# Block-diagonal products of the recurrent stage as 64x64 quarters, two blocks side by side

## What is computed

```python
def _layernorm(x, axis=-1, eps=1e-05):
    m = jnp.mean(x, axis=axis, keepdims=True)
    v = jnp.var(x, axis=axis, keepdims=True)
    return (x - m) / jnp.sqrt(v + eps)

xp = jnp.einsum('tbi,hi->tbh', x_in, W_ih) + b_ih + b_hh      # x_in = _layernorm(h)
def step(h, xp_t):
    h_new = jnp.tanh(xp_t + h @ W_hh.T)
    return (h_new, h_new)
...
h = h + _L1_attn_ref(_layernorm(h, axis=-1), ...)   # the recurrence
h = h + _L1_ffn_ref(_layernorm(h, axis=-1), ...)    # slice attention: logits, softmax, z, o
```

## Time and profile before

| | |
|---|---|
| median of 3 runs | 3429.57 us (3427.73 to 3431.83) |
| profiled execution | 3429.93 us, span 3428.1 us |
| busy: TensorE, VectorE, ScalarE, GpSimd | 88%, 74%, 63%, 58% of the span |
| TensorE's granted clock, mean | 0.953 of 2.4 GHz |
| stage of the change | about 1950 to 3428 us |

### The profile page before, as it was taken

How to read it: one execution, slowest core, us unless ns; L and a number is a source line. 1 busy time by engine, 2 the same in 40 slices (tenths; PEclk the granted TensorE clock), 3 DMA queues, 4 the chain that set the end, 5 groups by cost and what they waited for, 6 DMA issues and landing times. The chain is left out here.

```text
span 3428.1 us, 66757 instructions
## 1 busy us (share of the span) xinstructions
PE 3002.8 (88%) x24922; PEld 1681.2 (49%) x24922; DVE 2535.4 (74%) x3280; ACT 2168.8 (63%) x3082; POOL 1989.1 (58%) x1191
## 2 busy tenths in 40 slices
PE   8999999969898888974699758899999999999997
PEld 6777777735555555542244323344444444444444
DVE  7888888868888888872487447776767777777773
ACT  5666666658777777751244346676766666666662
POOL 7777777712788888886100256565656565655531
PEclk9999999989999999995899879999999999999999
DMA  1111111111212212111444311111111111111102
GB/s 45 39 39 40 39 39 39 35 53 44 62 55 68 58 52 58 53 40 38 156 150 150 114 36 34 32 52 45 52 46 51 46 51 46 51 47 47 48 26 52
DMA packets 208262, 191.09 MB, mean 56 GB/s; under 512 B 76381, under 2 KB 163398, under 8 KB 207562
## 3 DMA queue, kind: packets, MB, share of 16 engines
q1 hardware_dynamic: 173850, 142.95, 14.2%
q0 software_dynamic: 25600, 26.01, 3.0%
q10 hardware_dynamic: 8496, 17.87, 1.4%
HBM read 99.08 MB, written 87.65 MB: 54 GB/s over the span
## 5 line engine op out<-in xcount | busy, mean ns | idle before, releaser
L2363 POOL TENSOR_TENSOR E_w<-E_w,E_rs 128x1024 f32<-128x1024 f32 x200 | 409.0, 2045 | 528.6 <-DVE E_rs L2271 528.6
L2356 POOL DMA_INDIRECT E_row<-yb,P_gi x400 | 391.1, 978 | 399.2 <-POOLq L93 305.4
L647 POOL DMA_INDIRECT xb<-B_yt,P_gi x400 | 523.3, 1308 | 120.8 <-issue 114.1
L203 POOL TENSOR_TENSOR A_kmask<-A_ksb,A_pack_a 128x3584 f32<-128x3584 f32 x56 | 356.5, 6365 | 151.1 <-ACT A_ksb L350 151.1
L2256 DVE TENSOR_REDUCE E_mx<-E_lg 128x16 f32<-128x1024 f32 x200 | 242.3, 1211 | 203.5 <-PE E_lg L1919 198.7
L2155 ACT ACTIVATE E_w<-E_w 128x1024 f32<-128x1024 f32 x200 | 211.5, 1057 | 281.8 <-DVE E_w L2264 238.4
L2268 DVE TENSOR_REDUCE E_sm<-E_w 128x16 f32<-128x1024 f32 x200 | 243.8, 1219 | 121.4 <-ACT E_w L2155 110.2
L1950 PEld LDWEIGHTS E_wt<-S_pack_f,E_w 128*128 128x128 f32 (+1 forms) x1600 | 173.1, 143 | 198.6 <-issue 136.3
L432 DVE COPY A_vbd<-A_v 128x512 f32<-128x512 f32 x392 | 248.6, 680 | 15.2 <-PE A_v L290 15.0
L1950 PE MATMUL E_wt<-S_pack_f,E_w 128*128 128x128 f32 (+1 forms) x1600 | 220.9, 282 | 38.5 <-ACT E_mo L2203 25.9
L2264 DVE TENSOR_TENSOR E_w<-E_lg,E_mx 128x1024 f32<-128x1024 f32 x200 | 244.8, 1224 | 6.7
(11 more groups left out here) (322 smaller groups left out, 6972.3 us busy)
## 6 DMA issues: line engine op xcount, KB each, us to landing
R_xs<-xb SPq DMA_DIRECT2D x57, 256.0 KB, 2.7
yb<-R_ys SPq DMA_DIRECT2D x57, 256.0 KB, 2.0
B_x<-h SPq DMA_DIRECT2D x25, 512.0 KB
h<-B_hh SPq DMA_DIRECT2D x25, 512.0 KB
A_xg<-in_xw SPq DMA_DIRECT2D x56, 224.0 KB, 2.9
h<-A_res ACTq DMA_DIRECT2D x56, 224.0 KB, 2.0
E_hx<-h SPq DMA_DIRECT2D x48, 256.0 KB
out<-E_ob SPq DMA_DIRECT2D x96, 128.0 KB
```

The costliest lines, as they stand in the source:

```text
L203: nc.gpsimd.tensor_tensor(kmask[i % 2][:], bc(ksb[i % 2][:].unsqueeze(2), [128, J, H, Q]), bc(head_of_row[:].unsqueeze(1).unsqueeze(3), [1 ...
L647: pool.indirect_dma_start(out=xb, out_offset=bass.IndirectOffsetOnAxis(ap=routed.gi[0:k, c, b:b + 1], axis=0), in_=yt[c % LT][0:k, D * row ...
L2356: pool.indirect_dma_start(out=row[b % LR][:, k, i], out_offset=None, in_=yb, in_offset=bass.IndirectOffsetOnAxis(ap=idx[:, c, 2 * n + i:2 ...
L2363: TT(w3, w3, bc(rs[g % 3][:].unsqueeze(2), [128, 2 * SH, G]), ALU.mult).then_inc(w_done, 1)
```

## The change

`center_in(s)` and `inputs(s-1)` become one step, `center_and_inputs(s)`, and `variance(s)` and `variance_out(s-2)` become `variances(s)`. Each 128x128 product is issued as two 64x64 products on the quarters that are not zero. `along` takes rows i of the array to columns i, `across` takes rows i to columns 1-i, so that the result's halves are swapped; the centering of block s is issued across, its squares lie swapped in `sr`, and the variance, across again, puts them back. Both blocks' quarters are issued alternately, across to PI and along to PO. All semaphore waits of a joined step stand ahead of its first matmul. `center_and_inputs` stands ahead of product or turn_back, where `center_in` and `inputs` stood behind them; `first_hidden` stays behind them and gets a wait for `ih_done`.

```diff
-                def center_in(b):
-                    pe.wait_ge(x_done, b + 1)
-                    mm(PI[:, 0:wide(b)], center, x[b % LX][:, 0:wide(b)], start=True, stop=True).then_inc(cen_done, 1)
+                def across(i, to, weights, b, data, **kw):
+                    return mm(to[HALF[1 - i], 0:wide(b)], weights[HALF[i], HALF[i]], data[HALF[i], 0:wide(b)],
+                              start=True, skip_group_check=True, **kw)
+
+                def along(i, to, weights, b, data, **kw):
+                    return mm(to[HALF[i], 0:wide(b)], weights[HALF[i], HALF[i]], data[HALF[i], 0:wide(b)],
+                              start=True, skip_group_check=True, **kw)
+
+                def center_and_inputs(b):
+                    first, second = 0 <= b < BLOCKS, 0 <= b - 1 < BLOCKS
+                    if first:
+                        pe.wait_ge(x_done, b + 1)
+                    if second:
+                        pe.wait_ge(y_done, b)
+                        after(pe, hc_done, b - 1)
+                    for i in range(2):
+                        if first:
+                            cen = across(i, PI, center, b, x[b % LX], stop=True)
+                        if second:
+                            ih = along(i, PO, wih, b - 1, sr, stop=b - 1 < J)
+                    if first:
+                        cen.then_inc(cen_done, 1)
+                    if second:
+                        ih.then_inc(ih_done, 1)
...
-                def variance(b):
-                    pe.wait_ge(sq_done, b + 1)
-                    after(pe, yk_done, b - 2)
-                    mm(PI[:, 0:wide(b)], mean, sr[:, 0:wide(b)], start=True, stop=True).then_inc(var_done, 1)
-
-                def inputs(b):
-                    pe.wait_ge(y_done, b + 1)
-                    after(pe, hc_done, b)
-                    mm(PO[:, 0:wide(b)], wih, sr[:, 0:wide(b)], start=True, stop=b < J,
-                       skip_group_check=True).then_inc(ih_done, 1)
+                def variances(b):
+                    first, second = 0 <= b < BLOCKS, 0 <= b - 2 < BLOCKS
+                    if first:
+                        pe.wait_ge(sq_done, b + 1)
+                        after(pe, yk_done, b - 2)
+                    if second:
+                        pe.wait_ge(sq2_done, b - 1)
+                        pe.wait_ge(hc_done, b - 1)
+                        pe.wait_ge(tb_done, min(b, BLOCKS))
+                    for i in range(2):
+                        if first:
+                            var = across(i, PI, mean, b, sr, stop=True)
+                        if second:
+                            var2 = along(i, PO, meany, b - 2, sy[b % 2], stop=True)
...
                 def first_hidden(b):
                     if b >= J:
                         pe.wait_ge(tb_done, b - J + 1)
+                        pe.wait_ge(ih_done, b + 1)
...
-                def variance_out(b):
-                    pe.wait_ge(sq2_done, b + 1)
-                    pe.wait_ge(hc_done, b + 1)
-                    pe.wait_ge(tb_done, min(b + 2, BLOCKS))
-                    mm(PO[:, 0:wide(b)], meany, sy[b % 2][:, 0:wide(b)], start=True, stop=True).then_inc(var2_done, 1)
...
+                    if t == 1:
+                        center_and_inputs(s)
                     if begins(k):
                         product(k)
                     elif 0 <= k < TILES:
                         turn_back(k - 1)
                     if t == 1:
-                        at_block(center_in, s)
-                        at_block(inputs, s - 1)
                         at_block(first_hidden, s - 1)
...
                     if t == end:
-                        at_block(variance, s)
-                        at_block(variance_out, s - 2)
+                        variances(s)
```

More of the change, by code:

```diff
@@ L1878, in turn_y @@
                     last.then_inc(ty_done, 1)
-                def variance(b):
-                    pe.wait_ge(sq_done, b + 1)
-                    after(pe, yk_done, b - 2)
-                    mm(PI[:, 0:wide(b)], mean, sr[:, 0:wide(b)], start=True, stop=True).then_inc(var_done, 1)
-                def inputs(b):
-                    pe.wait_ge(y_done, b + 1)
-                    after(pe, hc_done, b)
-                    mm(PO[:, 0:wide(b)], wih, sr[:, 0:wide(b)], start=True, stop=b < J,
-                       skip_group_check=True).then_inc(ih_done, 1)
+                def variances(b):
[12 more added lines that the diff above has]
+                            var2 = along(i, PO, meany, b - 2, sy[b % 2], stop=True)
+                    if first:
+                        var.then_inc(var_done, 1)
+                    if second:
+                        var2.then_inc(var2_done, 1)
                 def first_hidden(b):
```

## The result

The changed kernel takes 3526.19 us (median of 4 runs, 3516.52 to 3527.94), the kernel before 3428.65 us beside it; the ratio is 1.0281, with a 95% interval of 1.0267 to 1.0295. Slower was forecast, but at 3482 us with an upper end of 3518; the loss is 98 us where 52 were expected. The profiled execution took 3527.57 us, its span is 3525.8.

A forecast was written before the change was run, and what follows sets the result against it. TensorE, by its streamed columns, was taken as the bound; 3429.9 + 24 (stalls less columns) - 5 (early blocks) + 33 (clock falls) = 3482 us. The 8-in-10 range was 3426 to 3518 us.

The forecast's parts named there:

- The bound and the saved columns: TensorE bounds by streamed columns; joined quarters save 0.8 us a turn and 0.6 a block end, about 80 us.
- the non-overlap rival: Quarters do not overlap: a joined step takes twice 1.02 us; 3590 us, or 3560 with the clock held; chance 0.04.
- The wait ahead of product: In block 28's turn t = 1 the joined step waits for `hold`, so TensorE stands for 2.46 us.
- Waits less columns: Stalls net of saved columns: +24 us in blocks 12 to 55, -5 us in blocks 4 to 11.
- One of the signs: Sign of being right: TensorE's busy time down by 60 us or more with the span longer.
- The faster rival: `hold` is not late at the joined step's start, so there is no stall: 3350 us; chance 0.12.
- its point of decision: At the joined step, saved columns win below a mean stall of some 0.9 us; ScalarE reaching square_out 1.5 us earlier.
- The clock: Granted clock halves after TensorE's new idle times: 21 falls of 38 at 1.6 us, +33 us; bounds 0 to +61.
- two idle times of the trace before: TensorE idle 2.1 us up to 2140.10, then clock 0.50 for 3.4 us; idle 1.9 us at 2183.80, clock stayed 1.00.
- The early blocks: Blocks 4 to 11: stall swallows only center, ends give 0.6 us each, -5 us; blocks 0 to 3: 0.
- its upper end: Own range to 3515 us at 38 falls, 6 us for the start; 8-in-10 range up to 3518 us.

The follow-up runs named there:

- the wait filled: Changed kernel with needless centering products issued into PI during the wait for `hold`, blocks 13 to 55 but every seventh: 3466.37 us, ratio 1.0128.
- The experiment with `hold` first: Changed kernel with `square_out` and `hold` ahead of the two copies of `keep_turned` in ScalarE's turn t = 1: 3416.63 us, ratio 0.9966.
- its ends apart: Changed kernel with variance (two crosswise quarters) and variance_out (whole) separate again, center and inputs still joined ahead of product: 3555.22 us, ratio 1.0386.

## Why the prediction was wrong

*The bound and the saved columns*: right. Four quarters run at once (0.81 us for 384 columns counted, 0.81 measured at an end), and some 80 us of columns were forecast to go and 76 went. The shared bank costs nothing, and the non-overlap rival is out. The Trainium skill (TensorEngine Tiling (Array Packing), "Gotcha 1: PSUM Pressure"), which the prediction cites, has it that different row tiles can't access one PSUM bank at the same time. For quarters at different columns this trace differs, with 0.81 us for a step that would take twice that if the two that write one bank took turns, and the measurement decides.

*The wait ahead of product*: right. 2.46 us of lateness was read off, and the same kind of turn shows 2.45: the joined step starts 3.51 us behind the logits, which take 1.06 (the idle time of 2.38 us in the row counts from the modelled end); the group was forecast near 100 us and measured at 108 in 49 waits. `hold` follows the exponential by the same 5.2 us. Waits less columns were +24 - 5 = 19 us; the trace leaves 22. With the wait filled the trace is 33 us longer than before behind the first logits, of which the clock has 4 (69 against 61 us at half clock); 29 us are left, of the same order. One of the signs was wrong, though: TensorE's busy time was to fall by 60 us or more and fell by 11, because work at half clock stays busy twice as long.

*The faster rival* was rightly given little, but its point of decision was reckoned wrong. The 8.3 us a pair is what the turns lose net of the saved columns, and not the stall, and a mean stall of 0.9 us leaves out what the ends save. With 0.8 us a block saved in the turn and 0.6 at the end, as the prediction counts, the point of decision is 1.4 us, the clock aside. So `hold` needed to come some 1.0 us earlier and not 1.5. The experiment with `hold` first moved it by 1.05 us, the waits came down to 1.3 us on average (57.3 us in 43), and the kernel went below the one before.

*The clock*: the step that failed, a term of the sum that was mis-sized. "I take somewhat over half, 21 falls: +33 us" came to 73 us, by the number of falls and by the price of one. Behind the first logits 45 stretches of low clock begin, against 13 before, 32 more where 21 were taken; and they cost 73 / 32 = 2.3 us each where 1.6 was taken, since some last 6.8 us and more, as the one at 2627.60. Of the 34 idle times of 2.2 to 2.7 us behind 2100 us, 33 were followed by a fall. With the measured clock term the sum gives 3430 + 19 + 73 = 3522 us, against 3526.

The sum stood on two idle times of the trace before, and the shorter of these, 1.9 us with the clock held, pulled the estimate down, though nearly all the new ones were longer than the longer of the two, 2.1 us, behind which it fell. That trace held more. Two further idle times, of 2.0 and 2.1 us, ended at 2116.2 and 2164.1, and right behind them stand these stretches (columns as in the earlier trace rows):

```profile
2116.20:2119.60 3.40, 3.38 (x10) 1.76 (x10) 2.61 (x4) 3.37 (x6) 2.27 (x2) 0.51 0.08 19
...
2164.10:2167.40 3.30, 3.29 (x8) 1.75 (x10) 2.61 (x4) 3.27 (x6) 2.18 (x2) 0.50 0.08 20
```

Behind 2100 us it has 13 idle times of 1.9 us or more that begin at full clock, and 10 of them have a fall in them or within 2 us behind. TensorE was busy for 50 us at half clock in its 13 stretches, a loss of 1.9 us for each. An estimate from these counts, 38 x 10/13 = 29 falls at 1.9 us, is +55 us and a sum of 3504: nearer, though still short.

The early blocks went the same way: -5 us was forecast for them from their joined ends, but the joined step there waits in one piece too, and tiles 0 to 24 became 9 us longer, with 37 us at half clock against 17. The range failed with the term: its upper end rested on one stretch of 3.4 us behind each of 38 idle times, 61 us. But stretches of 6.8 us had been there before too, and the early blocks, which were not among the 38, have their own.

## What to carry to other kernels

A step that joins two products waits for the later of their inputs, so before joining, read when each input is ready against the place at which TensorE reaches the step. Put the joined step where other work fills that wait, or move its producer forward on its own engine; here both together turned +2.8% into -1.3%. Price a new idle time of TensorE twice: for itself, and for the half clock behind it; one long idle time cost more than the same lateness with some work laid into it. And take that second price from all idle times of the trace that are as long, not from one or two.

## What the runs showed of the hardware

Needless matmuls in a wait made the kernel 50 to 60 us faster, with 69 us at half clock behind the first logits instead of 207. Counted over the ten traces taken on the first chips (the two kernels and the eight experiments), for idle times of TensorE behind 2100 us that began at full clock: behind 1.0 to 1.7 us the clock fell, during the idle time or within 2 us behind it, in 6 of 188 cases, behind 1.85 to 2.0 us in 27 of 37, behind 2.2 to 2.7 us in 58 of 73. The last are not uniform: 33 of 34 in the changed kernel, 19 of 32 with its ends apart. So in this stage the clock often fell behind 1.9 us without a matmul, and almost never behind 1.4 us. What tells the last two kernels apart is open. And two quarters that write one bank from different row halves, into different partitions, run in parallel: the first passes of four quarters started within 20 ns, and the step of eight records of 384 columns took 0.81 us.
